# Byte pairs through the DMA transpose and a GpSimd cast in a quantised attention loop on one Trainium2 core

## The reference

```
q = (x @ Wq + bq).reshape(1, B * N, H, hd)           # 2048 tokens, H = 16 heads, hd = 16
kv = (cond @ Wkv + bkv).reshape(1, -1, 2, H, hd)
...
q = _fq_sym(q, axis=-1)        # round(x / s) in -127..127, s = max|x| / 127
k = _fq_sym(k, axis=-1)
v = _fq_sym(v, axis=2)
attn = jnp.einsum('bhqd,bhkd->bhqk', q, k)
attn = jax.nn.softmax(attn.astype(jnp.float32), axis=-1)
attn = _fq_unsigned(attn, axis=-1)   # round(x / s) in 0..255, s = max / 255 of the row
out = jnp.einsum('bhqk,bhkd->bhqd', attn, v)
return out @ Wp + bp
```

## Time and profile before

| | us |
|---|---|
| median of 3 runs | 3039.45 (3037.06 to 3040.23) |
| the profiled execution's own time | 3038.51 |
| its span | 3036.7 |
| PE busy, share of the span | 2498.7 (82%) |
| DVE busy | 1932.5 (64%) |
| ACT busy | 1482.0 (49%) |
| POOL busy | 409.3 (13%) |

### The profile page before, as it was taken

The page is one execution under the profiler, slowest core; times in us unless marked ns, Lnnn a source line. Parts: engine busy times, 40 slices in busy tenths (PEclk is TensorE's granted clock), DMA queues, the critical chain, the costliest instruction groups (busy, mean ns, idle before and its releaser), DMA issues. The chain is left out here.

```text
span 3036.7 us, 50228 instructions
## 1 busy us (share of the span) xinstructions
PE 2498.7 (82%) x16570; PEld 1358.9 (45%) x16570; DVE 1932.5 (64%) x3686; ACT 1482.0 (49%) x2055; POOL 409.3 (13%) x454
## 2 busy tenths in 40 slices
PE   6874775999979999999664888787878865999998
PEld 3333554555547777777552222222222232444444
DVE  6995556667743333333456998888888845666665
ACT  5552332444433333333232776666666633666664
POOL 0001220111012222333133000000000001001100
PEclk9886776999979999999776555555555567999999
DMA  2000000000010000000000999999999940000001
GB/s 83 0 0 19 0 0 12 16 26 21 21 29 18 18 17 17 17 17 9 21 0 18 177 176 169 165 169 162 171 163 171 173 71 17 24 23 16 23 23 36
DMA packets 594876, 175.35 MB, mean 58 GB/s; under 512 B 548642, under 2 KB 594212, under 8 KB 594724
## 3 DMA queue, kind: packets, MB, share of 16 engines
q1 hardware_dynamic: 594724, 173.44, 29.6%
HBM read 37.07 MB, written 2.10 MB: 13 GB/s over the span
## 5 line engine op out<-in xcount | busy, mean ns | idle before, releaser
L1682 DVE TENSOR_SCALAR_CACHE_REDUCE ctxT<-psum,e_nsq 128x1024 f32<-128x1024 f32 x512 | 637.2, 1282 | 74.2 <-issue 54.1
L1651 PE MATMUL psum<-e_KT,e_Qs 48*128 48x512 bf16 x1024 | 519.9, 611 | 181.7 <-DVE ctxT L1682 151.0
L1703 ACT ACTIVATE xh<-ctxT,e_ebias 128x2048 uint16<-128x2048 f32 x128 | 256.2, 2002 | 134.0 <-DVE e_ebias L1686 134.0
L1703 ACT ACTIVATE xl<-ctxT,e_ebias 128x2048 uint16<-128x2048 f32 x128 | 256.2, 2002 | 119.2 <-DVE e_ebias L1686 119.2
L1651 PEld LDWEIGHTS psum<-e_KT,e_Qs 48*128 48x128 bf16 x1024 | 67.3, 104 | 415.8 <-issue 408.1
L103 PE MATMUL psum<-xh,d_WT 128*128 128x512 f16 x768 | 229.4, 381 | 2.6 <-DVE d_WT L1214 2.6
L1662 PEld LDWEIGHTS psum<-e_Vi,xnT 128*128 128x128 f16 x4096 | 129.5, 105 | 216.8 <-issue 216.8
L1233 DVE TENSOR_TENSOR d_ACC<-psum,d_ACC 128x512 f32<-128x512 f32 x128 | 82.5, 686 | 171.1 <-PE psum L1287 171.1
L103 PE MATMUL psum<-xh,f_WA 128*128 128x512 f16 x544 | 152.7, 383 | 13.9 <-DVEq L1896 11.8
L103 PE MATMUL psum<-xh,c_Wx 128*128 128x512 f16 x576 | 161.3, 383 | 0.8 <-DVE X L960 0.8
L1662 PE MATMUL psum<-e_Vi,xnT 128*128 128x16 f16 x4096 | 152.5, 175 | 8.1 <-DMA xnT<-xh 4.5
(11 more groups left out here) (312 smaller groups left out, 4965.9 us busy)
## 6 DMA issues: line engine op xcount, KB each, us to landing
d_Wn<-in_L_attn_w_qkv SPq DMA_DIRECT2D x16, 384.0 KB, 3.2
f_W<-in_L_ffn_w_routed SPq DMA_DIRECT2D x32, 176.0 KB, 2.5
ctx_rows<-in_ctx SPq DMA_DIRECT2D x1, 2048.0 KB, 8.6
X<-in_x SPq DMA_DIRECT2D x1, 2048.0 KB, 14.0
c_Wgu<-in_L_ffn_rg SPq DMA_DIRECT2D x16, 128.0 KB, 2.1
c_Wgu<-in_L_ffn_rw SPq DMA_DIRECT2D x16, 128.0 KB, 2.2
c_Wd<-in_L_ffn_rw SPq DMA_DIRECT2D x16, 128.0 KB, 2.2
d_Wn<-in_L_attn_w_gate SPq DMA_DIRECT2D x16, 128.0 KB, 3.0
```

Source lines behind the costliest of these rows:

```text
L1651: mm = pe.matmul(m.bank[b + q], Qs[rows, x.u // 2 % QSLOTS, :], KTt[rows, j // 2, (2 * hf + q) * BLK:(2 * hf + q + 1) * BLK], start=True, ...
L1682: dve.tensor_scalar(S32[:, sl, hf * HALF:(hf + 1) * HALF].rearrange("p (a b) -> p a b", a=2), m.psum[:, b:b + 2, :], nsq[:, ds(x.n(), 1)], ...
L1703: act.activation(e16[x.u % SLOTS], S32[:, x.u % 2, :], ACT.Exp, bias=ebias[:, x.u % 2:x.u % 2 + 1], scale=-1.0, accum_out=esum[:, ds(x.n() ...
```

## The change

In the second block:

- ScalarE writes the exponents as bytes (`e8`) instead of uint16. The DMA transpose sees two neighbouring bytes as one two-byte value, so it turns 128 x 1024 values instead of 128 x 2048 (into `P8`). So that neighbours in a row end up in two different key tiles, the first block stores `KTt` with the keys of two token tiles alternating.
- GpSimd takes the pairs apart: `unpack` reads `P8` as bytes, in order, and writes bf16 into `PT` (L1591 of the changed kernel). Of two neighbouring bytes the first goes to one key tile and the second to the next one, 256 bytes away. It runs LATE = 3 units behind. `Vi` is bf16 too, and the factor 2 to the power 24 is gone.
- GpSimd also makes `ebias`, which VectorE made before. `S32`, `mn` and `ebias` have 4 slots instead of 2.
- The ring `Qs` and its copies are gone; TensorE reads `QT` itself.
- All 256 units are written out with constant wait values; the hardware loop, its registers and `wait_apart` are gone from this block. TensorE's LAG is 7 instead of 6.

```diff
-        Vi = sb("Vi", [P, KT, H, HD], F16)
+        Vi = sb("Vi", [P, KT, H, HD], BF16)
...
-                            act.activation(KTt[:, :, ds(t * P, P)], m.bank[b + 1].bitcast(BF16)
-                                           .rearrange("p (a b) -> p a b", a=PR), ACT.Copy).then_inc(stored, 1)
+                            act.activation(KTt[:, :, ds(i * 2 * TPB * P + tt // 2 * 2 * P, 2 * P)]
+                                           .rearrange("p a (q b) -> p a q b", b=2)[:, :, :, tt % 2],
+                                           m.bank[b + 1].bitcast(BF16).rearrange("p (a b) -> p a b", a=PR),
+                                           ACT.Copy).then_inc(stored, 1)
...
-        BODY, SLOTS, LAG, QAHEAD, QSLOTS = 48, 4, 6, 3, 6
+        SLOTS, LAG, LATE = 4, 7, 3
...
-        PT = m.xnT[:, :, :].rearrange("p a b -> p (a b)").bitcast(F16).rearrange("p (s k q) -> p s k q", s=SLOTS, k=KT)
-        e16 = [x[:, :, :].rearrange("p a b -> p (a b)").bitcast(U16)[:, i * TOK:(i + 1) * TOK]
-               for x in (m.xh, m.xl) for i in range(2)]
...
+        S32 = [m.ctxT[:, 0, :], m.ctxT[:, 1, :], Smore[:, 0, :], Smore[:, 1, :]]
+        PT = m.xnT[:, :, :].rearrange("p a b -> p (a b)").bitcast(BF16).rearrange("p (s k q) -> p s k q", s=SLOTS, k=KT)
+        e8 = m.xh[:, :, :].rearrange("p a b -> p (a b)").bitcast(U8).rearrange("p (s k) -> p s k", s=SLOTS)
+        P8 = m.xl[:, :, :].rearrange("p a b -> p (a b)").bitcast(U16).rearrange("p (s c q) -> p s c q", s=SLOTS, c=KT // 2)
...
+                def unpack(n):
+                    sl = n % SLOTS
+                    pool.wait_ge(laid[sl], 16 * (n // SLOTS + 1))
+                    if n >= SLOTS:
+                        pool.wait_ge(mixed, n - SLOTS + 1)
+                    pool.tensor_copy(PT[:, sl, :, :].rearrange("p (c b) q -> p c q b", b=2),
+                                     P8[:, sl, :, :].rearrange("p c q -> p (c q)").bitcast(U8)
+                                     .rearrange("p (c q b) -> p c q b", c=KT // 2, b=2)).then_inc(unpacked, 1)
+
+                def step(n):
+                    if n < N:
+                        sl = n % SLOTS
+                        pool.wait_ge(score_out, 2 * n + 2)
+                        pool.tensor_scalar(ebias[:, sl:sl + 1], mn[:, sl, 0:1], mn[:, sl, 1:2], LN255,
+                                           ALU.min, ALU.add).then_inc(biased, 1)
+                    if n >= LATE:
+                        unpack(n - LATE)
+                loop(step, LATE)
...
-                    sp.dma_start_transpose(PT[:, x.u % SLOTS, :, :], e16[x.u % SLOTS].bitcast(F16)).then_inc(laid[x.u % SLOTS], 16)
+                    if n >= SLOTS:
+                        sp.wait_ge(unpacked, n - SLOTS + 1)
+                    sp.dma_start_transpose(P8[:, sl, :, :], e8[:, sl, :].bitcast(U16)).then_inc(laid[sl], 16)
...
-                    m.wait_apart(dve, score_out, x.n(1, 2) + 2)
-                    dve.tensor_scalar(ebias[:, sl:sl + 1], mn[:, sl, 0:1], mn[:, sl, 1:2], LN255,
-                                      ALU.min, ALU.add).then_inc(biased, 1)
```

More of the change, by code:

```diff
@@ L1375, in quantised_attention @@
     chain_s, vmaxed, vall = (m.sem(f"e_{n}") for n in ("chain", "vmax", "vall"))
-    q_here, scored, score_out, biased, exped, mixed, normed, chain2 = (m.sem(f"e_{n}") for n in (
-        "q_here", "scored", "score_out", "biased", "exped", "mixed", "normed", "chain2"))
+    scored, score_out, biased, exped, unpacked, mixed, normed, chain2 = (m.sem(f"e_{n}") for n in (
+        "scored", "score_out", "biased", "exped", "unpacked", "mixed", "normed", "chain2"))
     laid = [m.sem(f"e_laid{i}") for i in range(4)]
@@ L1607, in _ @@
             def _(pool):
[L1609 to L1622, removed]
@@ L1650, in score @@
+                        if c >= 3:
+                            pe.wait_ge(score_out, c - 2)
                         for q in range(2):
-                            mm = pe.matmul(m.bank[b + q], Qs[rows, x.u // 2 % QSLOTS, :],
+                            mm = pe.matmul(m.bank[pair_banks(c) + q], QT[rows, n // 2, :],
                                            KTt[rows, j // 2, (2 * hf + q) * BLK:(2 * hf + q + 1) * BLK],
@@ L1671, in _, with step @@
-                loop(pe, step, LAG)
+                def step(n):
+                    if n < N:
+                        score(n)
+                    if n >= LAG:
+                        mix(n - LAG)
+                loop(step, LAG)
             @block.vector
             def _(dve):
-                def step(x):
-                    sl = x.u % 2
-                    if x.at_least(2):
-                        m.wait_apart(dve, exped, x.n() - 1)
+                def step(n):
+                    sl = n % SLOTS
+                    if n >= SLOTS:
+                        dve.wait_ge(exped, n - SLOTS + 1)
@@ L1688, in _, with output @@
[L1688 removed]
+                loop(step)
             @block.scalar
             def _(act):
[L1692 to L1706 removed]
+                def output(n):
+                    t, half = n // H, n // 8 % 2
+                    act.wait_ge(mixed, n + 8)
+                    act.activation(Osb[:, t, half * P:(half + 1) * P], m.bank[6 + half][:, 0:P], ACT.Copy).then_inc(normed, 1)
@@ new lines, in step @@
+                def step(n):
+                    sl = n % SLOTS
+                    if n < N:
+                        act.wait_ge(biased, n + 1)
+                        if n >= SLOTS:
+                            act.wait_ge(laid[sl], 16 * (n // SLOTS))
+                        act.activation(e8[:, sl, :], S32[sl], ACT.Exp, bias=ebias[:, sl:sl + 1],
+                                       scale=-1.0, accum_out=esum[:, n:n + 1]).then_inc(exped, 1)
+                    done = n - LAG - 8
+                    if done >= 0 and done % 8 == 0:
@@ L1707, in step @@
                         output(done)
-                loop(act, step, LAG + 8)
+                loop(step, LAG + 8)
         rsum = sb("rsum", [P, N])
```

94 lines of the change are left out of this document (23 added, 71 removed).

## The result

| | us |
|---|---|
| changed kernel, median of 4 runs | 4722.07 (4720.18 to 4722.59) |
| kernel before, beside it | 3038.26 |
| ratio | 1.554 (95% interval 1.5513 to 1.5567) |
| span of the profiled execution | 4718.4 |

The prediction said 2874, with 2855 to 3290 as its range. The time lies outside of it, on the side of the rival "GpSimd's stores pay for the stride", and far beyond the 3292 that this rival was given at the most.

The account below looks back on a forecast made before the run. VectorE was taken to set the pace, everybody waiting for it. 255.5 x (3.110 - 2.46) = 166 us less, +1 at the end, takes 3038.5 to 2873.5, forecast as 2874; range 2855 to 3290.

Parts of the forecast that it names:

- GpSimd's stores pay for the stride: Slower rival, second block: cast 3.2 to 3.7 us, 3178 to 3292 us in all, put at 3280; chance 0.33.
- the price of GpSimd's cast: Second block: casting 2048 elements on GpSimd takes 1.89 us, linear in the elements whatever the type.
- VectorE, 2.42 us: Second block: VectorE keeps only the two reduces of a unit, 2 x 1.21 = 2.42 us.
- 0.51 to 0.68 us a unit: VectorE's time beside the reduces, to go: 0.51 in 64 written-out units, 0.68 in 192 looped ones.
- the turns: Hardware loop turns before a VectorE reduce, to go: two of 4 us each.
- TensorE, 2.41: Second block: TensorE's matmuls at 1.2 GHz need 2.41 us a unit, nearly as slow as VectorE.
- The coupling with VectorE: TensorE and VectorE share three bank pairs; 0.94 of matmul plus 1.28 of reduce fit in 3.63 us.
- the 2.46 given: Period a unit, put a little above the 2.41 to 2.42 us of three engines.
- GpSimd's rest: GpSimd's bias of 0.25 us and gaps beside the cast; its unit 2.30 to 2.54 us, taken as 2.42.
- DMA: Transposes in the block: bytes halve, share 1.01 becomes at most half, about 1.5 us a unit; share near 0.6 expected.
- 2.92 a unit: Upper bound for the DMA transposes if the price goes by descriptor and not by byte.
- First block: Storing `KTt` with a step of 4 bytes, on an engine that idles there, costs nothing.

Follow-up runs that it names:

- p1_shapes: Kernel before plus a first block where GpSimd, VectorE and ScalarE copy or cast 2048 elements alone in different shapes; 3161.23 us, the change's cast shape 9.20 us on GpSimd.
- e1_loops: Changed kernel with the cast's loops exchanged, so bytes are read with a step of 2 and stores run on; median 2861.08 us, ratio 0.9415.
- p2_steps: Kernel before plus a first block where GpSimd, then VectorE, copy 2048 elements alone with the step between stores, then reads, swept; 3179.57 us.
- p4_words: Kernel before plus a first block storing 2048 elements on GpSimd, then VectorE: byte pairs and fours, bf16 pairs and a run starting mid-word, lone bf16; 3083.68 us.
- e6_bias_vector: Changed kernel with the cast's loops exchanged and the bias back on VectorE, 4 slots kept; median 2922.61 us, ratio 0.9606.
- e8_plain_waits: Kernel before with all 256 units written out and each `wait_apart` of this loop made a plain wait; 2926.55 us, ratio 0.9628.
- e7_unrolled: Kernel before with only the loop changed: all 256 units written out with constant numbers; median 2997.55 us, ratio 0.9862.
- e5_bias_vector_far: Changed kernel with only the bias moved back to VectorE, the slow cast kept; 4559.66 us (one run).
- e2_no_bytes: Changed kernel without the bytes: uint16 exponents, two-byte transpose, fp16, LAG 6, no cast, GpSimd making only the bias; median 2925.25 us, ratio 0.9628.

## Why the prediction was wrong, and what of it held

**The step that failed** is the price of GpSimd's cast: "I take the linear value, because every GpSimd row lies on it". Every one of those rows stores its elements one behind the other, so they say nothing about stores 256 bytes apart. The cast took 9.234 us, not 1.89 (p1_shapes shows it alone, and the order of its two loops makes the kernel 4722 or 2861: e1_loops). 2048 opened lines x 4.4 ns + 0.19 = 9.2.

**The rival had the mechanism** and the right chain (TensorE for the cast, ScalarE for the bias), and the point from which it decides, a cast of 2.7 us, was passed. Its size was off by more than two: it came from a read, 1.70 ns an element on VectorE, and a store that fills no word costs 4.4 on GpSimd (p2_steps, p4_words). For a strided read on GpSimd its 3.2 to 3.7 us would have been right (3.62 to 3.84 in p2_steps). With a cast of 9.20 its own sum, 9.20 + 0.25 + 0.16 = 9.61 us a unit, gives 3038.5 + 255.5 x (9.61 - 3.11) = 4699, against the measured 4720. That rows of VectorE were taken for GpSimd made it worse: VectorE's lone bf16 stores cost 2.2 ns.

**VectorE, 2.42 us:** held. 2.41 in e1_loops. That 0.51 to 0.68 us a unit would go was right as a sum, but not what it was made of: the bias itself is 0.25 (e6_bias_vector), the rest is `wait_apart` (e8_plain_waits) and the register waits of the loop (e7_unrolled). Of the turns it counted two, and put 5 us down to the first units; most of that is a third turn:

```profile
2256.53 1.28 DVE L1682 TENSOR_SCALAR_CACHE_REDUCE ctxT<-psum,e_nsq 128x1024 f32<-128x1024 f32 x1 [3.98 <-issue]
```

**TensorE, 2.41:** held, it has no gap in e1_loops. The coupling with VectorE costs nothing there: the unit takes 2.41, not the 2.46 given, which is 255.5 x 0.05 = 13 us, the whole distance from 2874 to 2861.

**GpSimd's rest:** the bias takes 0.29, not 0.25, and GpSimd is busy for 90% of 2.41, which is 2.18. With the 0.06 between bias and cast that is below the 2.30 to 2.54 of the forecast; it changed nothing, as GpSimd isn't the bound there. Beside a slow cast the bias costs 0.64 (e5_bias_vector_far).

**DMA:** share 0.59 as forecast. That 1.01 was a near-limit was misread (1.18 in e8_plain_waits), and the bound "2.92 a unit" for two-byte transposes was too high: 2.66.

**First block:** "nothing" was nearly right. ScalarE's store of `KTt` takes 1.31 instead of 1.02 us, 16 times, 4.7 us on an engine that idles there. It follows the same rule: 256 lines x 4.4 + 0.19 = 1.32.

```profile
L1466 ACT ACTIVATE e_KT<-psum 128x1024 bf16 x16 | 21.0, 1313 | 0.0
```

**Where the gain of the mended version comes from.** Writing out 41 us (3038 to 2998), plain waits 71 (to 2927). The last 66 need two things at once, because VectorE with the bias and the two-byte transposes both stand at 2.66 us:

| | two-byte transpose | bytes |
|---|---|---|
| bias on VectorE | 2926.6 (e8_plain_waits) | 2922.6 (e6_bias_vector) |
| bias on GpSimd | 2925.3 (e2_no_bytes) | 2861.1 (e1_loops) |

The bias alone is worth 1 us, the bytes alone 4, neither of them clear of the spread of these runs (2923.3 to 2928.2 in e8_plain_waits, 2914.3 to 2924.3 in e6_bias_vector). (e8_plain_waits also has two slots and `Qs`, the others four and none.) Which of the engines' `wait_apart`s cost the 71 us wasn't taken apart.

## What to carry to other kernels

Before a copy or cast with rearranged sides is costed, count the 16-byte lines that its stores open and look whether they fill 4-byte words: put the stride on the read, or order the loops so that stores run on. A read has its price too once its step is large (3.77 us with 16 bytes, against 9.23 for the store and 1.89 for one run). A price read from contiguous rows bounds nothing for a strided one, and one from a read doesn't bound a store; where the change hangs on such an instruction, the range has to say so. When two resources stand at the same time a unit, an experiment that relieves one of them shows nothing, and only both together show what each is worth.

## What the runs showed that was not expected

- Lone 2-byte stores cost 4.4 ns on GpSimd and ScalarE for each opened 16-byte line, and 1-byte ones the same on GpSimd; on GpSimd pairs that fill a word cost at most 1.7 (1.92 instead of 9.28 us for the same 2048 elements).
- The same lone stores cost VectorE half: 4.7 us, but 5.32 in the change's own shape.
- Reads of bytes with a step of 2 are free on GpSimd (1.890 and 1.891 us).
- Two of the slow casts in a row on GpSimd overlap by 0.41 us, and a short instruction between them takes twice its duration (0.64 for 0.29). It isn't so for every pair: two memsets of 3.51 us in p1_shapes start 3.45 apart, an overlap of 0.06.
- Waits followed by a semaphore increment of their own, on all engines together: 71 us in 256 units, 0.28 us a unit.
